# Staged W1, hidden products made the other way round, one seed in four on ScalarE, and half of W1's staging copied by ScalarE

## The reference

```python
w1 = W1[language_ids]                                # 512 x 128 for each batch
w2 = W2[language_ids]                                # 128 x 512
h = relu(x @ w1 + b1[language_ids])                  # 128 x 128
adapted = h @ w2 + b2[language_ids]                  # 128 x 512
y = x + adapted
normed = (y - mean(y)) * rsqrt(var(y) + 1e-5)        # over the 512 columns
out = x + normed * gamma[language_ids] + beta[language_ids]
```

## Time and profile before

| what | value |
|---|---|
| device time, median of 3 runs (lowest, highest) | 325.59 us (325.28, 325.63) |
| profiled execution: span from first to last instruction | 323.8 us |
| PE, DVE, ACT, POOL busy over the span | 301.9, 307.6, 230.4, 185.7 us |
| mean granted PE clock over the span | 0.969 |
| traffic with HBM | 41.62 MB read, 33.55 MB written |

### The profile page before, as it was taken

How to read it: one execution, slowest core, us unless ns; L and a number is a source line. 1 busy time by engine, 2 the same in 40 slices (tenths; PEclk the granted TensorE clock), 3 DMA queues, 4 the chain that set the end, 5 groups by cost and what they waited for, 6 DMA issues and landing times. The chain is left out here.

```text
span 323.8 us, 8068 instructions
## 1 busy us (share of the span) xinstructions
PE 301.9 (93%) x2200; PEld 272.8 (84%) x2200; DVE 307.6 (95%) x679; ACT 230.4 (71%) x541; POOL 185.7 (57%) x217
## 2 busy tenths in 40 slices
PE   1659999999999999999999999999999999999962
PEld 1239899999999999999999999999999999999941
DVE  5687999999999999999999999999999999999996
ACT  3956677777777777877778777787777877778752
POOL 2960755556655566555665556655566555665553
PEclk9877999999999999999999999999999999999995
DMA  5999988766766667676776676766667666433324
GB/s 160 302 356 428 379 291 273 236 228 231 257 232 227 228 229 263 223 233 226 230 256 232 228 231 227 261 236 221 231 225 262 221 234 232 160 132 134 130 108 152
DMA packets 41711, 75.69 MB, mean 234 GB/s; under 512 B 2253, under 2 KB 7404, under 8 KB 41542
## 3 DMA queue, kind: packets, MB, share of 16 engines
q1 hardware_dynamic: 41571, 75.04, 68.5%
q10 hardware_dynamic: 99, 0.14, 0.1%
HBM read 41.62 MB, written 33.55 MB: 232 GB/s over the span
## 5 line engine op out<-in xcount | busy, mean ns | idle before, releaser
L295 POOL TENSOR_TENSOR x_io<-x_io,beta_all 128x512 f32<-128x512 f32 x128 | 161.2, 1280 | 0.0
L401 PE MATMUL ps_h<-w_all,x_T 128*128 x1024 | 137.0, 284 | 0.0
L401 PEld LDWEIGHTS ps_h<-w_all,x_T 128*128 128x128 f32 x1024 | 126.1, 194 | 1.6
L345 ACT ACTIVATE cut<-ps_y,row_sum 128x512 bf16<-128x512 f32 x128 | 88.0, 688 | 24.0 <-PE ps_y L428 24.0
L572 DVE SCALAR_TENSOR_TENSOR x_io<-ps_y,rstd,x_io 128x512 f32<-128x512 f32 x128 | 90.2, 747 | 2.5 <-DVE rstd L564 0.3
L559 DVE SCALAR_TENSOR_TENSOR ps_y<-ps_y,mean,gamma_all 128x512 f32<-128x512 f32 x128 | 90.8, 754 | 0.8 <-ACT cut L345 0.6
L292 POOL TENSOR_TENSOR mean<-row_sum,over_h 128x2 f32<-128x2 f32 x64 | 12.9, 201 | 125.6 <-DVE ps_y L540 113.6
L540 DVE SCALAR_TENSOR_TENSOR ps_y<-x_io,b_all 128x512 f32<-128x512 f32 x124 | 83.1, 713 | 0.0
L393 PE MATMUL ps_T<-identity,x_io 128*128 128x128 f32 x512 | 68.2, 277 | 10.0 <-DMA x_io<-in_x 10.0
L393 PEld LDWEIGHTS ps_T<-identity,x_io 128*128 128x128 f32 x512 | 61.1, 143 | 19.1 <-issue 10.4
L322 ACT COPY x_T<-ps_T 128x1024 f32<-128x1024 f32 x64 | 63.7, 995 | 8.2 <-PE ps_T L393 8.2
(11 more groups left out here) (60 smaller groups left out, 173.6 us busy)
## 6 DMA issues: line engine op xcount, KB each, us to landing
x_io<-in_x SPq DMA_DIRECT2D x64, 512.0 KB, 4.4
out<-x_io SPq DMA_DIRECT2D x63, 512.0 KB, 3.0
x_io<-in_L_cond_W SPq DMA_DIRECT2D x5, 512.0 KB, 7.2
w_all<-in_L_cond_W SPq DMA_DIRECT2D x5, 512.0 KB, 8.9
b_all<-in_L_cond_b SPq DMA_DIRECT2D x1, 2560.0 KB, 15.7
out<-x_io SPq DMA_DIRECT2D x2, 256.0 KB, 2.0
x_io<-in_L_cond_gamma SPq DMA_DIRECT2D x1, 60.0 KB
x_io<-in_L_cond_beta ACTq DMA_DIRECT2D x1, 60.0 KB
```

The source lines that it names most:

```text
L295: nc.gpsimd.tensor_tensor(x_slot(t), x_slot(t), of_lang(beta_all, langs[b]), ALU.add)\
L345: nc.scalar.activation(squares[:, t % 2, :], ps_y[t % Y_BANKS][:, :], ACT.Square, scale=-float(H), bias=stat(row_sum, t), accum_out=stat(s ...
L401: last = nc.tensor.matmul(part, x_T[:, t % 4, c, :], w1_all[:, bass.ds(lang, 1), c, :].rearrange("p o a -> p (o a)"), start=False, stop=(c ...
```

## The change

1. **W1 is staged.** A buffer `w1_stage` has slots for four pairs, two tiles each. SP fills them six pairs ahead with transfers: for pairs 0 to 5 both tiles from HBM, from pair 6 on only the first tile, from `w1_all`. The second tile from pair 6 on is copied by ACT (`copy_w1`), which needs a language load of its own on ACT's queue.
2. **The first products are made the other way round.** The staged W1 is the weight and `x_T` moves, so `ps_h` (now two banks) has h already turned. `turn_h`, `copy_h`, `h_rows` and `ps_hT` go; `high_h` takes the ReLU straight from `ps_h`, and `low_h` takes the maximum with zero. b1 comes in with one bf16 matmul for the pair, 256 columns.
3. **One seed in four on ACT.** From tile 7 on, each tile t with t % 4 == 3 is seeded by ACT (x alone, with its row sum), and its b2 is added by one bf16 matmul of 512 columns on PE. So that the row sum is right, b2's rows are centred at startup (three small ACT instructions).
4. **Order and sizes.** `FIRST` goes from 3 to 2, x has 10 pair slots and not 12, `H_PAIRS` goes from 6 to 3; DVE seeds before `low_h`; SP's startup order is another.

```diff
+        def by_scalar(t):
+            return t % 4 == 3 and t >= 2 * EARLY
...
+            def stage_w1(q):
+                langs = langs_of(sp, q)
+                if q >= STAGE_PAIRS:
+                    sp.wait_ge(h_summed, q - STAGE_PAIRS + 1)
+                if q >= STAGE_HBM:
+                    sp.wait_ge(s_w1, 16 * W_CHUNKS)
+                table = w1_rows if q < STAGE_HBM else w1_all
+                sp.dma_start(w1_stage[:, 2 * (q % STAGE_PAIRS), :, :], table[:, bass.ds(langs[0], 1), :, :])\
+                    .then_inc(w1_staged[q % STAGE_PAIRS], 16)
+                if q < STAGE_HBM:
+                    sp.dma_start(w1_stage[:, 2 * (q % STAGE_PAIRS) + 1, :, :], table[:, bass.ds(langs[1], 1), :, :])\
+                        .then_inc(w1_second_staged[q % STAGE_PAIRS], 16)
...
+            sp.wait_ge(ids_ready, 1)
+            stage_w1(0)
+            load_w2(0)
+            load_w2(1)
+            load_x(1)
+            stage_w1(1)
+            for n in range(2, W_CHUNKS):
                 load_w2(n)
+            load_x(2)
+            stage_w1(2)
+            sp.dma_start(b2_all[:, :, :], b2.partition_broadcast(128)).then_inc(s_b2, 16)
+            load_x(3)
+            stage_w1(3)
...
             for p in range(PAIRS - 1):
+                if p + STAGE_AHEAD < PAIRS:
+                    stage_w1(p + STAGE_AHEAD)
                 sp.wait_ge(out_ready, 2 * p + 2)
...
             def high_h(p):
-                act.wait_ge(h_turned, p + 1)
+                act.wait_ge(h_summed, p + 1)
                 if p >= H_PAIRS:
                     act.wait_ge(adapted, 2 * (p - H_PAIRS) + 2)
-                nc.scalar.copy(flat(h_high[:, p % H_PAIRS, :, :]), pair_of(ps_hT)).then_inc(h_high_ready, 1)
+                nc.scalar.activation(flat(h_high[:, p % H_PAIRS, :, :]), pair_of(ps_h[p % 2]), ACT.Relu)\
+                    .then_inc(h_high_ready, 1)
...
+            def seed(t):
+                act.wait_ge(x_loaded[t // 2 % X_PAIRS], x_loads(t // 2))
+                act.wait_ge(out_ready, t - Y_BANKS + 1)
+                nc.scalar.activation(ps_y[t % Y_BANKS][:, :], x_slot(t), ACT.Identity,
+                                     accum_out=stat(row_sum, t)).then_inc(seeded_act, 1)
+
+            def copy_w1(q):
+                lang = langs_of(act, q)[1]
+                if q == STAGE_HBM:
+                    act.wait_ge(s_w1, 16 * W_CHUNKS)
+                act.wait_ge(h_summed, q - STAGE_PAIRS + 1)
+                nc.scalar.copy(w1_stage[:, 2 * (q % STAGE_PAIRS) + 1, :, :].rearrange("p c a -> p (c a)"),
+                               w1_all[:, bass.ds(lang, 1), :, :].rearrange("p o c a -> p (o c a)")).then_inc(w1_copied, 1)
+
             def step(p):
                 if p < PAIRS - 1:
                     copy_x(p + 1)
-                if p > 0:
-                    high_h(p - 1)
-                copy_h(p)
+                t = 2 * (p - FIRST) + 3
+                if by_scalar(t):
+                    seed(t)
+                high_h(p)
+                q = p + STAGE_AHEAD - FIRST
+                if STAGE_HBM <= q < PAIRS:
+                    copy_w1(q)
...
+            def first_products(p):
+                bank = pair_of(ps_h[p % 2])
+                if p >= 2:
+                    pe.wait_ge(h_low_ready, p - 1)
+                nc.tensor.matmul(bank.rearrange("a (b s) -> a b s", b=2), b1_parts[:, :],
+                                 is_lang[:, 2 * p:2 * p + 2].unsqueeze(2).broadcast_to([128, 2, S]), start=True, stop=True)
+                pe.wait_ge(w1_staged[p % STAGE_PAIRS], 16 * (p // STAGE_PAIRS + 1))
+                if p < STAGE_HBM:
+                    pe.wait_ge(w1_second_staged[p % STAGE_PAIRS], 16 * (p // STAGE_PAIRS + 1))
+                else:
+                    pe.wait_ge(w1_copied, p - STAGE_HBM + 1)
                 for b in range(2):
+                    for c in range(C):
+                        last = nc.tensor.matmul(bank[:, b * S:(b + 1) * S],
+                                                w1_stage[:, 2 * (p % STAGE_PAIRS) + b, c, :],
+                                                x_T[:, (2 * p + b) % 4, c, :],
+                                                start=False, stop=False, skip_group_check=True)
+                last.then_inc(h_summed, 1)
...
-                pe.wait_ge(seeded, t + 1)
+                wait_seed(pe, t)
+                if by_scalar(t):
+                    nc.tensor.matmul(bank, is_lang[:, t:t + 1].broadcast_to([128, S]), parts[:, 2 * H:3 * H],
+                                     start=False, stop=False, skip_group_check=True)
...
                     t = 2 * n + b
+                    if by_scalar(t):
+                        continue
...
-                if p is not None:
-                    low_h(p)
                 if n + 2 < PAIRS:
                     seed_pair(n + 2, langs[n + 2])
+                    low_h(n + 2)
```

More of the change, by code:

```diff
@@ L13 @@
 LN_EPS = 1e-5
-SLOTS = 24
+SLOTS = 20
 Y_BANKS = 4
-H_PAIRS = 6
-FIRST = 3
+H_PAIRS = 3
+STAGE_PAIRS = 4
+STAGE_AHEAD = 6
+STAGE_HBM = 6
+FIRST = 2
 EARLY = 2
@@ L89, in build @@
         row_sum = sb("row_sum", [128, SLOTS], F32)
-        mean = sb("mean", [128, SLOTS], F32)
+        neg_mean = sb("neg_mean", [128, SLOTS], F32)
         sq_sum = sb("sq_sum", [128, SLOTS], F32)
@@ L96, in build @@
         ps_T = psum("ps_T", [128, 2, C, S], F32)
-        ps_h = psum("ps_h", [128, H], F32)
-        ps_hT = psum("ps_hT", [128, H], F32)
+        ps_h = [psum(f"ps_h{i}", [128, H], F32) for i in range(2)]
         ps_y = [psum(f"ps_y{i}", [128, H], F32) for i in range(Y_BANKS)]
@@ L107, in build @@
         s_w1 = sem("s_w1")
+        w1_staged = [sem(f"w1_staged{i}") for i in range(STAGE_PAIRS)]
+        w1_second_staged = [sem(f"w1_second_staged{i}") for i in range(STAGE_PAIRS)]
+        w1_copied = sem("w1_copied")
         s_w2 = [sem(f"s_w2_{n}") for n in range(W_CHUNKS)]
@@ L163, in spread_to, with scalar_seeds, vector_seeds, wait_seed @@
             return (gamma_all if n < L else beta_all)[:, n % L, :]
+        def by_scalar(t):
+            return t % 4 == 3 and t >= 2 * EARLY
+        def scalar_seeds(t):
+            return len([u for u in range(t + 1) if by_scalar(u)])
+        def vector_seeds(t):
+            return t + 1 - scalar_seeds(t)
+        def wait_seed(engine, t):
+            if by_scalar(t):
+                engine.wait_ge(seeded_act, scalar_seeds(t))
+            else:
+                engine.wait_ge(seeded, vector_seeds(t))
         def x_slot(t):
@@ L302, in _ @@
             for n in range(PAIRS):
-                add_beta(n)
+                langs = langs_of(pool, n)
+                mean_of_pair(n)
+                for b in range(2):
+                    add_beta(2 * n + b, langs[b])
         @block.scalar
@@ L371, in _ @@
             high_w2(2)
-            copy_h(0)
-            copy_x(2)
             high_h(0)
             high_w2(3)
-            copy_h(1)
+            copy_x(2)
+            high_h(1)
             high_w2(4)
-            step(2)
+            act.wait_ge(ids_ready, 1)
             for p in range(FIRST, PAIRS):
@@ L381, in _ @@
                 step(p)
-            square_pair(PAIRS - FIRST)
-            high_h(PAIRS - 1)
-            for n in range(PAIRS - FIRST + 1, PAIRS):
+            for n in range(PAIRS - FIRST, PAIRS):
                 square_pair(n)
+                if n + 1 < PAIRS and by_scalar(2 * n + 3):
+                    seed(2 * n + 3)
         @block.tensor
@@ L465, in _ @@
                     turn_x(2 * p + 3)
-                if p > 0:
-                    turn_h(p - 1)
-                for b in range(2):
-                    first_product(2 * p + b, langs[p][b])
+                first_products(p)
                 if p < PAIRS - 1:
@@ L479, in _ @@
                     second_product(2 * n + b, langs[n][b])
-                if n == PAIRS - FIRST:
-                    turn_h(PAIRS - 1)
         @block.vector
```

135 lines of the change are left out of this document (69 added, 66 removed).

## The result

The changed kernel takes 333.81 us (median of 4 runs, 333.25 to 335.35) against 325.58 before: ratio 1.0267, interval 1.0243 to 1.0291. The prediction said 316.4 and faster; the time lies above its range. The span of the profiled execution is 332.0 us, 17.4 above the forecast span of 314.6.

The account below looks back on a forecast made before the run. PE bounded the kernel, DVE just behind; afterwards PE's wait for ACT's seed would set the step. Startup 34.0 + 62 x 4.36 - 0.87 + end 11.1 = 314.6 us span, plus 1.8 = 316.4 median; range 310 to 325.

Parts of the forecast that it names:

- the 34.0 of the sum: Startup: first second product at 34.0 us instead of 35.0, with 33 and 38 as ends.
- 4.36 a step: Loop: average step with a 0.15 us stall of PE for ACT's seed every two steps, against 4.49 before.
- Rival C: Startup: x or W1 stages late behind 512-byte rows, first second product at 38 us; median 320.4; chance 0.10.
- PE's own work: PE in the loop: 4.17 us without an ACT seed, 4.40 with one, 4.28 a step on average.
- rival A: Loop: load hidden or ACT's seed otherwise in time, so PE's 4.28 sets the step; median 311.4; chance 0.22.
- DVE, the step that failed: DVE in the loop: one seed in four goes, at most 4.16 us a pair on average, below PE.
- ACT's loop and the load: ACT: language load 0.60 behind high_h's wait, copy_w1 0.75 after high_h; seed 0.15 us late for PE every two steps.
- POOL's row: POOL's startup register instructions for L295, at 33.6 after a mean let go at 33.68: queue instructions don't pass a waiting one.
- Rival B: Loop: ACT's load 0.95, seed too late, 4.535 a step; median 327.2; balance at a load of 0.90; chance 0.15.
- The added transfers: DMA: one more 256 KB transfer a pair raises the share from 0.67 to at most 0.84, hidden.
- The end: After the last first product: 11.1 us to the end of the span, against 15.6 before.
- The prediction's sum of the kernel before: Check on the old kernel's span: 35.0 + 61 x 4.49 - 0.87 + 15.6, given as 323.8 us.

Follow-up runs that it names:

- the mended kernel: Another name for first_beta_before_mean: the changed kernel with POOL's order altered for odd pairs; 319.37 us.
- first_beta_before_mean: Changed kernel, but POOL adds the first tile's beta of an odd pair before the mean and the wait for ACT's seed; 319.37 us, ratio 0.9808.
- beta_second_load: first_beta_before_mean plus a second language load on ACT per step, kept alive by a one-column copy, ahead of the W1 copy; 335.56 us, ratio 1.0327.
- beta_and_dma: first_beta_before_mean with both staged W1 tiles by SP's transfer, no W1 copy or language load on ACT; 327.4 us, ratio 1.007.
- before_clash: Kernel before the change, plus one POOL wait so beta is added only once DVE turns to its two seeds; 345.45 us, ratio 1.0613.
- rows_and_beta: first_beta_before_mean with W1's HBM rows 2 KB long, not 512 bytes, and transposes taking x's columns with a step of four; 320.75 us, ratio 0.9827.

## Why the prediction was wrong

**The start of the second product: its reason held, its reach did not.** The first second product came at 32.14, better than the 34.0 of the sum. The sum then went on at 4.36 a step from there. Missing was the sentence that x of pairs 4 and 5 is due within two steps and stands behind the table. "Four slots' worth of stage transfers" was put down as a loss and had no price of its own; with them W1 went in 12 tiles more than before, in short rows. Rival C had this mechanism ("x or W1 stages come late behind 512-byte rows"), with 4 us where the start lost 6.6, but placed it ahead of the first second product. Its sign, a transfer that lets PE go between 22 and 45 us, came at 44.21.

**PE's own work: right.** 4.17 forecast for a short step, 4.17 measured; 4.40 for a long step's own work, 4.40 in the mended kernel, where PE stands at 4.28 on average, rival A's step. The b1 matmul of 256 columns costs 0.11 (182.84 to 182.95), as assumed.

**DVE, the step that failed.** "Two seeds cost 185.28 - 184.02 = 1.26, so one is 0.63, every second pair: 4.48 less 0.32 is at most 4.16 on average" took a seed's duration as fixed, and with it DVE was put below PE. Two pairs on DVE took 8.91 us (from 179.54 to 188.45, the scaling of one pair to that of the next but one), 4.46 each. By the sum it would be 8.32; the 0.72 that one seed takes longer is the difference, but for 0.13. "POOL's work is unchanged, its waits split in two" was true, and there was the miss: moved in time, the same additions meet DVE's seed. In the kernel before they ended ahead of the next seeds, so no row of its loop shows the price. Rows of its startup have the sign of it (DVE's and POOL's timelines of the kernel before):

```profile
18.19 3.98 DVE L523 SCALAR_TENSOR_TENSOR w_low<-x_io,w_neg_mean,w_high 128x512 fp32r<-128x512 f32 x4
...
33.45 1.41 DVE L523 SCALAR_TENSOR_TENSOR w_low<-x_io,w_neg_mean,w_high 128x512 fp32r<-128x512 f32 x2
```

```profile
18.89 1.70 POOL L277 TENSOR_TENSOR b_rows<-b_rows,b_cut 30x512 f32<-30x512 f32 x1
```

With two large operands in SBUF, DVE's instruction takes 1.0 each (3.98 for four) while POOL works and 0.7 each while POOL stands still. That POOL's addition is what made the four longer is argued from the loop; no run tried it at the startup. The Trainium skill has the rule, on the page "SBUF — State Buffer", section "Who interferes with whom": a DVE instruction with two SBUF inputs and a GpSimd instruction that reads SBUF use one port pair, one at a time for a whole instruction, and the one that issues second stands until the first is done. By that rule the trace agrees: 1.41 for a seed that POOL was ahead of, 0.48 for a mean that DVE was ahead of, and no change for the output instructions (one of the two large inputs in PSUM) under POOL's additions. The prediction weighed no such rival; it would have been 0.7 on every second pair: 4.16 + 0.35 = 4.51 a step, close to the 4.53 measured.

**ACT's loop and the load: right in form, not what set the end.** `copy_w1` starts 1.00 after `high_h` in one step of the timeline and 0.64 in the next (180.55 to 181.55, 184.94 to 185.58); the load on ACT has a median of 0.804 where I took 0.60, with a longest of 1.779. The copy takes 0.53 from start to start. But PE's steps there are stretched by DVE, and ACT's seed comes early enough. That the load stands behind the wait of `high_h` fits: in the mended kernel `copy_w1` starts 0.62 after a `high_h` that had waited (185.71 to 186.33) and 0.44 after one that had not (181.51 to 181.95). POOL's row, on which the prediction rested this, can't tell which wait held the queue, since two stand ahead of that mean in the list. In the mended kernel the load has a median of 0.494, and the loop fits under PE's 4.28:

```profile
L173 ACTq TENSOR_LOAD <-lang_ids x58: 487/804/1779, 38.1 to 302.2; - x58
```

```profile
L173 ACTq TENSOR_LOAD <-lang_ids x58: 482/494/2097, 40.5 to 288.3; - x58
```

The rows are from the loads by source line, of the kernel after and of first_beta_before_mean. Rival B's point of balance, a load of 0.90, was not reached by the median; beta_second_load shows what lies behind it.

**The added transfers: hidden in the loop, not at the start.** A share of 0.84 was the bound, 0.87 was measured, and no wait for a transfer stands in PE's loop. At 1.00 (beta_and_dma) such waits come.

**The end** took 11.7 for 11.1. The prediction's sum of the kernel before, as printed, gives 323.6 and not 323.8, as its step is rounded to 4.49; the forecast doesn't rest on it.

Put right, the sum of the mended kernel closes: the second product of pair 2 at 45.6, then 60 steps at 4.33 less 0.87, then 11.9 give 316.4, for a span of 316.3. The profiled execution took 318.12 us, 1.8 above its span as in the kernel before; the median of 319.37 is higher because the run of 583.19 counts in it. What stays open: that run itself, why the start varies by 3.7 us between kernels with one startup order, and whether 2 KB rows could be had without the transposes' price, which was not tried.

## What to carry to other kernels

When work is moved between engines, the work that waits for it moves too: list for every shifted instruction what else it now runs beside, and look in the trace, startup included, for the same kind of instruction with and without that company. Instructions of DVE and GpSimd that both read two SBUF operands are to be placed so that they don't overlap, by order in the list rather than by luck. At a start, follow each engine two or three steps past the first result and ask when each of its inputs is issued.

## What the runs showed of the hardware, unexpected

- The exclusion between DVE and POOL holds for very short instructions too: a POOL product of 128x2 took 0.48 and not 0.20 behind a DVE seed of 0.69.
- A load of two numbers from SBUF into a register had medians from 0.49 to 1.59 us and a longest of 2.55, by engine and kernel. Busy transfers alone don't explain it: in before_clash, at a DMA share of 0.64 (60 to 300 us), POOL's and DVE's medians are 1.30 and 1.28, where before, at 0.67, they were 0.85 and 0.58.
- Rows of 512 bytes seem to cost at the start: 293 against 386 GB/s from 30 to 45 us, at DMA shares of 1.09 and 1.05. The Trainium skill's page "DMA: Bandwidth & Descriptors", section "Specifications", gives 512 bytes as enough for line rate; the trace does not agree for this mix.
- Weights of a transpose that are read with a step of four f32 cost about 0.01 us more for each of the eight (0.08 a step in rows_and_beta); the mean of their weight loads went from 143 to 208 ns.
